# Fill units cut into chunks at the scan's waits, scan rows gathered instead of scattered, and the next image's statistics taken from a load of their own

## The reference

```
def _gn(v, G=32, eps=1e-05):      # mean and variance over a group's 16 channels and all pixels
    ...
# L0: channels plus 25 correlations of each pixel with its 5x5 neighbours, 1x1 convolution, relu
# L1: state-space layer
xz = silu(in_proj_w @ x + b)                    # 1536 channels: x_ssm, res, gate
xf = silu(depthwise_conv3(x_ssm))               # along the tokens
dt, B_t, C_t = split(dbc_w @ xf)                # 2 heads x (1 + 8 + 8); dt = softplus
perm = argsort of a score of the pixels, one per head   # the scan's order of the tokens
h_t = exp(dt_t * A) * h_(t-1) + dt_t * B_t * x_t ;  y_t = h_t . C_t + D * x_t    # in perm's order
y   = y[inverse perm] * silu(gate) + res
out = silu(out_proj_w @ y + b)
x = x + L0(_gn(x));  x = x + L1(_gn(x));  x = x + L2(_gn(x));  x = x + L3(_gn(x))   # L2, L3: 1x1 convolutions
```

## Time and profile before

| | us |
|---|---|
| median of 3 executions | 1927.8 (1924.85 to 1931.48) |
| the profiled execution: its time | 1925.98 |
| its span | 1924.2 |
| TensorE busy | 1734.3 |
| VectorE busy | 1092.5 |
| ScalarE busy | 859.8 |
| GpSimd busy | 413.3 |

### The profile page before, as it was taken

How to read it: one execution, slowest core, us unless ns; L and a number is a source line. 1 busy time by engine, 2 the same in 40 slices (tenths; PEclk the granted TensorE clock), 3 DMA queues, 4 the chain that set the end, 5 groups by cost and what they waited for, 6 DMA issues and landing times.

```text
span 1924.2 us, 23528 instructions
## 1 busy us (share of the span) xinstructions
PE 1734.3 (90%) x8558; PEld 948.2 (49%) x8558; DVE 1092.5 (57%) x2115; ACT 859.8 (45%) x1045; POOL 413.3 (21%) x419
## 2 busy tenths in 40 slices
PE   0639899999999999999999999999999999999977
PEld 0315455455545555455454565454554555545533
DVE  4664747535765358544675257654475356753544
ACT  3335424554344634455334544346245553445431
POOL 0210330223110330113301322103301132113310
PEclk9859999999999999999999999999999999999988
DMA  6200231113211231013311232012410133112201
GB/s 238 58 1 8 92 126 36 44 37 102 91 34 44 94 128 29 23 44 109 108 37 44 72 94 78 19 45 94 132 37 22 43 101 104 37 44 94 72 17 44
DMA packets 120455, 128.61 MB, mean 67 GB/s; under 512 B 51715, under 2 KB 100931, under 8 KB 120078
## 3 DMA queue, kind: packets, MB, share of 16 engines
q1 hardware_dynamic: 105998, 90.58, 15.0%
q0 software_dynamic: 12288, 34.68, 5.5%
q10 hardware_dynamic: 2048, 1.76, 0.3%
HBM read 66.99 MB, written 60.01 MB: 66 GB/s over the span
## 4 chain that ended last, share of the span: by engine, by line
PE 55%; DVE 13%; issue 11%; ACT 8%; DMA 7%; POOL 3%; SPq 2%; DVEq 0%; POOLq 0%; ACTq 0%
PE bank L1278 53%; DMA rows<-d_scan 3%; POOL d_scan L416 3%; ACT buf_a L508 2%; ACT work L511 2%; DVE bn L783 2%; DMA x_odd<-in_x 1%; DMA d_scan<-rows,rank 1%; ACT work L543 1%; DMA x_even<-in_x 1%; PE bank L1413 1%; DVE mv L1176 1%; DVE gate L1066 1%; DMA w_out<-in_woutt 1%; SPq L293 1%
## 5 line engine op out<-in xcount | busy, mean ns | idle before, releaser
L1278 PE MATMUL bank<-buf_a,win_hi 128*128 128x512 f16 x1536 | 460.7, 382 | 11.3 <-DVE buf_a L829 8.1
L1278 PE MATMUL bank<-buf_b,w_hi 128*128 128x512 f16 x1024 | 307.8, 383 | 18.3 <-DVE buf_b L829 17.4
L1278 PE MATMUL bank<-buf_a,win_lo 128*128 128x512 f16 x768 | 293.1, 382 | 0.0
L1278 PEld LDWEIGHTS bank<-buf_a,win_hi 128*128 128x128 f16 x1536 | 149.0, 98 | 200.6 <-issue 26.6
L1278 PE MATMUL bank<-gate,w_out 128*128 128x512 f32 x512 | 230.3, 598 | 9.7 <-DVE gate L1068 9.7
L416 POOL DMA_INDIRECT d_scan<-rows,rank x128 | 125.7, 982 | 357.1 <-DVE rows L1044 310.7
L1278 PE MATMUL bank<-buf_b,w_lo 128*128 128x512 f16 x512 | 195.7, 382 | 0.0
L1278 PEld LDWEIGHTS bank<-buf_b,w_hi 128*128 128x128 f16 x1024 | 100.1, 99 | 138.4 <-DVE buf_b L829 19.2
L433 POOL DMA_INDIRECT rows<-d_y,rank x128 | 124.8, 975 | 146.7 <-DMA d_y<-buf_b 106.0
L1278 PE MATMUL bank<-buf_a,w_hi 128*128 128x512 f16 x512 | 155.0, 385 | 0.0
L1278 PEld LDWEIGHTS bank<-gate,w_out 128*128 128x128 f32 x512 | 94.0, 191 | 114.1 <-issue 98.9
(11 more groups left out here) (226 smaller groups left out, 2771.7 us busy)
## 6 DMA issues: line engine op xcount, KB each, us to landing
rows<-d_scan SPq DMA_DIRECT2D x16, 1092.0 KB, 5.8
d_y<-buf_b SPq DMA_DIRECT2D x64, 256.0 KB, 2.1
d_gram<-rows SPq DMA_DIRECT2D x32, 260.0 KB, 2.6
x_even<-in_x SPq DMA_DIRECT2D x16, 512.0 KB, 5.4
...
```

What stands on the lines that cost most here:

```text
L1278: return eng.matmul(out, lhsT, rhs, start=start, stop=stop, skip_group_check=True, **kw)
```

## The change

1. TensorE's fill units can be laid in pieces of one chunk (`piece(n)`). Of the 18 units that stood ahead of the scan 17 are left; pieces stand in `scan_inner`, after `scan_y`, and three ahead of the output parts, where a whole unit stood between them. ScalarE evicts 8 units ahead of the scan and one more between two exponentials of head 1. The last unit uses bank 1 instead of 4.
2. The 256 columns of the scan rows are stored to `d_scan` in token order as soon as they are copied, the 17 others after row_ready, by SyncE's queue; GpSimd gathers whole rows by `order`, the inverse of rank. `order` is made once per head: GpSimd scatters the token numbers by rank, SyncE's queue reads them back.
3. The statistics of the next image are taken from four loads of their own into `normed`, two ahead of row_ready and two behind it on VectorE; group sum, variance and bias move along. The loads into X[1 - z] stay where they are; ScalarE normalises three of its four chunks ahead of the output evictions.

```diff
+parts["token"] = np.repeat(n[:, :, None], 2, axis=2)
...
-in_bank = (3, 4, 6, 1, 2, 1, 2, 1) + (2, 1) * 7 + (2, 4)
+in_bank = (3, 4, 6, 1, 2, 1, 2, 1) + (2, 1) * 8
...
     around = bass.AP(d_norm.tensor, d_norm.offset, [[1, P], [P, NT], [1, 2 * REACH + 1]])
     eng.dma_start(near, around).then_inc(s["norm_in"], 16)
+def order_in(h):
+    eng.wait_ge(s[f"order_out{h}"], 16 * NT)
+    eng.dma_start(order_f[:, h], d_order[h].rearrange("(c p) r -> p c r", p=P)).then_inc(s[f"order_in{h}"], 16)
 def image(m, z, last=False):
     first = is_first(m)
+    def x_store(h):
+        wait(eng, "tok_ev", m, 2 * h + 2)
+        eng.dma_start(d_scan[h].rearrange("(c p) r -> p c r", p=P)[:, :, 0:DH], rows4[:, h, :, 0:DH]).then_inc(s[f"x_stored{h}"], 16)
...
+    def early(k):
+        eng.dma_start(normed[:, k % 2, :], d["x"][bass.ds(m + 1, 1), k * P:(k + 1) * P, :].rearrange("a p n -> (a p) n")).then_inc(s["early_in"], 16)
...
+    if not last:
+        wait(eng, "gn_split1", m, KC)
+        early(0)
+        early(1)
+    x_store(0)
+    if not last:
+        wait(eng, "gn_raw0", m + 1, 4)
+        early(2)
+        early(3)
+    wait(eng, "row_ready", m, 1)
     for h in range(HEADS):
-        wait(eng, f"scattered{h}", m, 16 * NT)
-        eng.dma_start(rows4[:, h], d_scan[h].rearrange("(c p) r -> p c r", p=P)).then_inc(s[f"scanrows{h}"], 16)
+        eng.dma_start(d_scan[h].rearrange("(c p) r -> p c r", p=P)[:, :, DH:ROW], rows4[:, h, :, DH:ROW]).then_inc(s[f"p_stored{h}"], 16)
+    x_store(1)
+    if first:
+        order_in(1)
...
             wait(eng, "y_ev", m, 4 * h + j + 1)
...
+order_in(0)
...
+def order_out(h):
+    eng.wait_ge(s["p_rank"], h + 1)
+    eng.nop(nofuse=True)
+    for t in range(NT):
+        eng.indirect_dma_start(d_order[h], bass.IndirectOffsetOnAxis(ap=rank[:, h, t:t + 1], axis=0),
+                               const("token")[:, 2 * t:2 * t + 2], None).then_inc(s[f"order_out{h}"], 16)
...
-    wait(eng, "row_ready", m, 1)
-    wait(eng, "tok_ev", m, KC)
-    eng.nop(nofuse=True)
     for h in range(HEADS):
+        if h and not last:
+            rstd(m + 1, 0)
+        if first and h:
+            order_out(h)
         if first:
-            eng.wait_ge(s["p_rank"], h + 1)
-            eng.nop(nofuse=True)
-        for t in range(NT):
-            eng.indirect_dma_start(d_scan[h], bass.IndirectOffsetOnAxis(ap=rank[:, h, t:t + 1], axis=0),
-                                   rows4[:, h, t, :], None).then_inc(s[f"scattered{h}"], 16)
+            eng.wait_ge(s[f"order_in{h}"], 16)
+            eng.tensor_copy(order[:, h, :], order_f[:, h, :, 0]).then_inc(s["order_ev"], 1)
+            eng.wait_ge(s["order_ev"], h + 1)
+        wait(eng, f"x_stored{h}", m, 16)
+        wait(eng, f"p_stored{h}", m, 16)
+        eng.nop(nofuse=True)
+        for c in range(NT):
+            eng.indirect_dma_start(rows4[:, h, c, :], None, d_scan[h],
+                                   bass.IndirectOffsetOnAxis(ap=order[:, h, c:c + 1], axis=0)).then_inc(s[f"gathered{h}"], 16)
     def diagonal(h):
...
     if not last:
...
 l0_adds(0, 0)
 rstd(0, 1)
...
         wait(eng, f"gn_bias{g}", m, 1)
+    if k == 0 and g == 0:
...
-    filler(9)
+    filler(8)
...
     scan_exp(1, 1)
+    filler(1)
     scan_y(0, 0)
...
+        normalize(m + 1, 0, 0, X[1 - z])
+        normalize(m + 1, 0, 1, X[1 - z])
+        normalize(m + 1, 0, 2, X[1 - z])
         for u in range(3):
             out_evac(m, u)
-        normalize(m + 1, 0, 0, X[1 - z])
-        out_evac(m, 3)
-        normalize(m + 1, 0, 1, X[1 - z])
-        out_evac(m, 4)
-        normalize(m + 1, 0, 2, X[1 - z])
-        out_evac(m, 5)
         normalize(m + 1, 0, 3, X[1 - z])
-        out_evac(m, 6)
-        out_evac(m, 7)
+        for u in range(3, 8):
+            out_evac(m, u)
...
+def early_stats(m, part):
+    wait(eng, "early_in", m - 1, 32 * (part + 1))
+    for k in (2 * part, 2 * part + 1):
+        for half in range(2):
+            eng.bn_stats(bn[0][:, k, half, :], normed[:, k % 2, half * HALF:(half + 1) * HALF]).then_inc(s["gn_raw0"], 1)
+    if part:
+        for k in range(KC):
+            aggregate(m, 0, k, 8 + k)
...
+    if not last:
+        early_stats(m + 1, 0)
     wait(eng, "dbc_mm", m, 1)
     dbc = rows4[:, :, :, DH:ROW]
...
+    if not last:
+        early_stats(m + 1, 1)
+        moments(m + 1, 0)
+        variance(m + 1, 0)
     scan_masks(m, 0)
     if not first:
         eng.wait_ge(s["x_out"], m * per["x_out"])
     scan_factors(m, 0, z)
     scan_masks(m, 1)
+    if not last:
+        bias(m + 1, 0)
     scan_states(m, 0)
     scan_factors(m, 1, z)
...
-    if not last:
-        input_stats(m + 1, 1 - z)
     gated(4, 2, 0)
     gated(5, 3, 0)
     if not last:
-        variance(m + 1, 0)
+        split(m + 1, 0, 0)
     gated(6, 2, 1)
     gated(7, 3, 1)
     if not last:
-        bias(m + 1, 0)
+        split(m + 1, 0, 1)
     for u in range(8):
         out_unit(m, z, u)
-        if u > 2 and u < 7 and not last:
-            split(m + 1, 0, u - 3)
+        if u == 0 and not last:
+            split(m + 1, 0, 2)
+        if u == 2 and not last:
+            split(m + 1, 0, 3)
         if u:
             out_stats(m, z, u - 1)
...
     dt, _, cst_c = scan_columns(h)
-    wait(eng, f"scanrows{h}", m, 16)
+    wait(eng, f"gathered{h}", m, 16 * NT)
...
-    def in_unit(q, ready=lambda k: None):
+    def in_step(q, k):
         part, o, c = in_unit_at(q)
-        if q < 5 and q != 2 and not first:
-            wait(eng, "l3_add", m - 1, (3, 4, 0, 6, 7)[q])
-        elif q > 4:
-            wait(eng, "in_evac", m, q - 1)
-        for k in range(KC):
-            ready(k)
-            ins = passes("in", (0, 2, 1)[part] * KC + o, 1, k, c, in_bank[q], k == 0, k == KC - 1)
-        ins.then_inc(s["in_done"], 1)
+        if k == 0:
+            if q < 5 and q != 2 and not first:
+                wait(eng, "l3_add", m - 1, (3, 4, 0, 6, 7)[q])
+            elif q > 4:
+                wait(eng, "in_evac", m, q - 1)
+        if q == 0:
+            wait(eng, "gn_split1", m, k + 1)
+        ins = passes("in", (0, 2, 1)[part] * KC + o, 1, k, c, in_bank[q], k == 0, k == KC - 1)
+        if k == KC - 1:
+            ins.then_inc(s["in_done"], 1)
+    steps = iter([(q, k) for q in range(24) for k in range(KC)])
...
+        piece(KC * n)
     if first:
         eng.wait_ge(s["w_lo_in"], KC)
-    in_unit(0, lambda k: wait(eng, "gn_split1", m, k + 1))
-    fill = iter(range(1, 24))
-    def filler(n):
-        for _ in range(n):
-            in_unit(next(fill))
+    filler(1)
     def tokens(k):
...
     tokens(3)
-    filler(9)
+    filler(5)
+    if not last:
+        gn_sum(m + 1, 0)
+    filler(3)
     def scan_sums(h):
...
                     ins.then_inc(s["fac_tp"], 1)
+        piece(1)
         for half in range(2):
             wait(eng, "fac_ptq", m, 4 * h + (3 if half == 0 else 4))
...
         far = FAR_GROUP[h] * S
         for c in range(NT - 1):
+            if c == 4 and h == 0:
+                piece(1)
             if c >= 4 and c % 2 == 0:
                 wait(eng, "h_st", m, 7 * h + c - 2)
...
     filler(1)
     scan_y(0)
+    piece(1)
     scan_inner(1)
     filler(2)
     scan_y(1)
+    piece(1)
     def y_chunk(k, half):
...
         y_chunk(k, 1)
+    piece(3)
     wait(eng, "in_evac", m, 23)
     for k in (0, 1):
         wait(eng, "y_res", m, 2 * k + 1)
-        for u in range(3):
-            out_part(u, k)
-    filler(1)
+        out_part(0, k)
+        out_part(2, k)
+        if k == 0:
+            wait(eng, "in_evac", m, 24)
+        out_part(1, k)
+    wait(eng, "y_res", m, 3)
     out_part(3, 0)
     out_part(3, 1)
     y_chunk(2, 0)
-    wait(eng, "in_evac", m, 24)
     y_chunk(3, 0)
     wait(eng, "y_res", m, 4)
     out_part(4, 0)
     out_part(4, 1)
-    if not last:
-        gn_sum(m + 1, 0)
     wait(eng, "y_res", m, 5)
     out_part(0, 2)
     out_part(1, 2)
```

More of the change, by code:

```diff
@@ L128, in build @@
         rank = sb("rank", [P, HEADS, NT], I32)
+        order = sb("order", [P, HEADS, NT], I32)
+        order_f = sb("order_f", [P, HEADS, NT, 2])
         deq8 = sb("deq8", [P, HEADS, T8])
@@ L191, in build @@
         d_scan = [nc.dram_tensor(f"d_scan{h}", (N, ROW), F32, kind="Internal").ap() for h in range(HEADS)]
+        d_order = [nc.dram_tensor(f"d_order{h}", (N, 2), F32, kind="Internal").ap() for h in range(HEADS)]
         d_score = nc.dram_tensor("d_score", (P, HEADS * NT), F32, kind="Internal").ap()
@@ L203, in build @@
             l0_done l0_evac l0_add_pool l0_add_dve in_done in_evac out_done out_evac out_add l2_done l2_add l3_done l3_add
-            conv_pad conv_mac conv_act tok_mm tok_ev dbc_mm sp_z sp_dve sp_act row_ready scattered0 scattered1 scanrows0 scanrows1
+            conv_pad conv_mac conv_act tok_mm tok_ev dbc_mm sp_z sp_dve sp_act row_ready x_stored0 x_stored1 p_stored0 p_stored1 gathered0 gathered1 order_out0 order_out1 order_in0 order_in1 order_ev
```

(32 more changed lines are left out.)

14 lines of the change are left out of this document (7 added, 7 removed).

## The result

| | before | changed |
|---|---|---|
| median of 5 executions, us | 1927.0 (1923.6 to 1931.5) | 1946.0 (1941.3 to 1947.3) |
| ratio to before | | 1.0092, 95% interval 1.0070 to 1.0113 |
| the profiled execution: time | 1926.0 | 1942.6 |
| its span | 1924.2 | 1940.8 |
| TensorE busy | 1734.3 | 1735.8 |

The account below looks back on a forecast made before the run. TensorE's order bounds the kernel (busy 213.9 of 222 us an image). Terms 13.7 - 7.2 - 2.4 + 0.5 + 7.5 = +12.1 on 1926.0 gave 1938.1, for the median 1939, range 1924 to 1955.

Parts of the forecast that it names:

- The first piece waits for the eviction: In scan_inner(0), TensorE stands 3.15 us until ScalarE evicts the 18th unit; products start 3.3 us later.
- The clock: After the new 3.15 us wait the granted clock drops in five of eight images, 1.5 us each: +7.5 us.
- The first image: Group sum waits 15 us for moments, head 1's order chain delays c = 4 by 15.4; whole image +13.7 us.
- The store: Scan rows: storing 17 columns after row_ready, then gathering, brings head 0's masks 4 us earlier; term -3.2 us an image.
- I take 3, near the small pieces: Scan rows: the 17-column store lands in 3 us, between bounds of 2.5 and 5.8.
- the new store is slow: Rival: the 17-column store takes 5.8 us, TensorE waits 2.1 more in seven images, 1954 us; chance 0.15.
- no wait is left: Scan rows: TensorE no longer waits for head 0's masks, which come with 0.7 us of slack.
- Their fourth lands 0.7 us before TensorE asks: Ahead of the output projection: the fourth y gather lands 0.7 us before TensorE needs it.
- Covers come out as meant: Rival: the 18th unit's bank is free when scan_inner(0)'s first piece asks; median 1909 us; chance 0.1.

Follow-up runs that it names:

- Experiment 1: Changed kernel with the first piece in scan_inner(0) moved from ahead of the products to c = 4; 1915.3 us.
- experiment 2: Changed kernel with ScalarE's eviction of the 20th unit moved from between head 1's exponentials to behind head 1's factors; 1929.0 us.
- experiment 5: Changed kernel with the edits of Experiment 1, experiment 2 and experiment 3 together; 1897.0 us.
- experiment 3: Changed kernel, first image only: head 1's rows scattered by rank again, statistics behind head 0's masks, group sum and bias behind the scan; 1938.2 us.
- experiment 4: Changed kernel with only the first image's statistics moved behind head 0's masks, group sum and bias behind the scan; 1937.7 us.
- the best one: The kernel of experiment 5 with the additions of experiment 7 and experiment 8 together; 1889.8 us.
- experiment 8: Experiment 5's kernel; in the first image head 0's states go ahead of head 1's masks, head 1's order behind the diagonal blocks; 1894.7 us.
- experiment 7: Experiment 5's kernel with the 1 MB store of head 1's columns held until head 0's 17 columns have landed; 1893.3 us.

## Why the prediction was right, and where it was not

**The first piece waits for the eviction: right, to 0.04 us.** It was read off ScalarE's order and the earlier trace rows that TensorE would stand 3.15 us; it stood 3.11. `scan_sums(0)` to `scan_inner(1)` should grow by 5.0 and grew by 4.7 where the clock held. Experiments 1 and 2 took the two causes out one by one.

**The clock: right in kind, and charged too high.** The forecast had five of eight images by 1.5 us, 7.5 in all. It was four of eight. In three of them the stretch is 1.3 to 1.6 us longer, 4.5 in all; in the first image it costs nothing, since TensorE waits for VectorE at c = 4 anyway. When the wait went, none of images 2 to 8 had it in this place (experiments 1 and 5). The table of stretches of the changed kernel, behind the wait in the third, the fourth and the fifth image (columns as in the earlier trace rows):

```profile
684.00:686.00 2.00, 2.00 (x7) 1.35 (x8) 1.14 (x5) 1.88 (x2) 0.00 (x0) 0.50 0.00 0
907.00:909.00 2.00, 1.86 (x14) 1.61 (x15) 1.29 (x5) 1.98 (x3) 0.12 (x1) 1.00 0.00 0
...
1131.00:1133.00 2.00, 2.00 (x11) 2.00 (x11) 0.00 (x0) 0.64 (x1) 0.00 (x0) 0.50 0.00 0
```

After the same wait of 3.11 us the granted clock is 0.50 in two of them, the level of 1.2 GHz, and 1.00 in the other. With this wait in every image, kernels differ in how many images drop: three of images 2 to 8 here, five in each of experiments 3 and 4, and all but the last in experiment 2. That may be part of why single executions of these kernels scatter more than those of the best one (1888.2 to 1891.5); it was not tested. The wait of 3.11 is not the only one that does it. Behind waits of 1.52, 1.63 and 2.11 us ahead of `scan_sums(0)` the clock fell too (experiments 2, 8 and 5), and behind 1.53 to 1.72 in the changed kernel and 2.02 in experiment 7 it held.

**The first image: right in mechanism, 1.1 us too long.** Masks of head 1 were put at 241.3 and came at 240.5, c = 4 at 243.7 and came at 242.8, the group sum's wait at 15 and was 15.14. The ranks ended at 205.9, 1.5 earlier than before. The 13.7 of the sum is for the whole image: 15.4 up to c = 4, 1.7 for the y copies, and the rest is won behind the y transposes. Up to these, where the table above cuts, it says +17.1, and +16.0 came (14.5 at c = 4, 1.5 behind it).

**The store: the term that was mis-sized.** The step "I take 3, near the small pieces" failed. It landed in 5.8, the upper bound, and the first gather came 5.3 to 6.1 us behind row_ready in images 2 to 8, where 3.7 had been forecast. That was the rival "the new store is slow", whose size was right and whose price of 15 us was not: it came to 10. TensorE waits 0.8 to 1.7 us ahead of `scan_sums(0)` in images 2 to 8, where "no wait is left" had been said; their sum is 9.7 us, and y transposes to `scan_sums(0)` shrank by 5.1 us where the terms made 6.5. The rule of the Trainium skill cited beside that rival (DMA: Bandwidth & Descriptors, Specifications), that a transfer below 512 B is read, modified and written, is neither shown nor excluded by these runs. Pieces of 512 B made the kernel slower, but brought 7.5 times the bytes; experiment 7 found 0.5 us of head 0's delay in the 1 MB store behind it. What makes up the rest stays open.

**The y gathers.** "Their fourth lands 0.7 us before TensorE asks" held in four of the eight images: in the second, third, fourth and sixth the wait is 0.61, 0.38, 1.95 and 0.71. In the other four no wait is shown. The four make 3.7 us, which no term of the sum has.

**The rivals.** "Covers come out as meant" gave 1909 on the condition that ScalarE had evicted in time. Experiment 1 is close to that condition: it came to 1915, where the changed kernel stood at 1941; 6.9 us of waits for scan rows and y rows are still in it. The rule of the Trainium skill cited in the prediction (ScalarE: Activation LUTs, What ACT_TABLE_LOAD costs), a drain of 1.38 us on top of each load, would by the estimate there have made some 20 us more; here the trace again shows 1.28 and an activation right behind.

In sum, the profiled execution was forecast at 1938.1 and took 1942.6. By the landmarks above, with the prediction's terms added up for the same stretches:

| us against before | forecast | measured |
|---|---|---|
| first image up to its y transposes | +17.1 | +16.0 |
| y transposes to `scan_sums(0)`, seven times | -46.2 | -35.6 |
| `scan_sums(0)` to `scan_inner(1)`, seven times, with the clock | +42.5 | +37.3 |
| last image's y transposes to the end | -1.3 | -1.0 |
| sum | +12.1 | +16.6 |

So the 4.5 us between them are the rest of two larger errors: 10.6 too much won ahead of the scan (the store, and the y gathers), and 5.2 too much lost in it (3 of them the clock). That they nearly cancel is luck. The median lies 3.4 us over the profiled execution, where 1.8 had been carried over from before, and 1938.1 and 1.8 make 1939.9, not 1939 (in the same way the first rival's sum makes 1910, not 1909). These two are the rest of the distance from 1939 to 1946.
